# Joint expert tiles for two batches in a gated cross-attention and mixture-of-experts kernel

## The reference

```
x = x + tanh(g_xattn) * align(ctx, layernorm(x))          # x1
logits = layernorm(x1) @ gate_w.T
w, sel = top_k(logits, 2); w = softmax(w)
out = x1 + tanh(g_ffn) * sum_k w[k] * (layernorm(x1) @ expert_w[sel[k]].T)
```

## Time and profile before

| | |
|---|---|
| median of 3 runs | 618.98 us (618.24 to 619.47) |
| profiled execution | 618.64 us, its span 616.7 us |
| busy: PE, DVE, ACT, POOL | 492.8, 280.0, 280.7, 240.3 us |
| expert tiles | 78, gathers 277.8 to 588.6 us |

### The profile page before, as it was taken

How to read it: one execution, slowest core, us unless ns; L and a number is a source line. 1 busy time by engine, 2 the same in 40 slices (tenths; PEclk the granted TensorE clock), 3 DMA queues, 4 the chain that set the end, 5 groups by cost and what they waited for, 6 DMA issues and landing times.

```text
span 616.7 us, 7978 instructions
## 1 busy us (share of the span) xinstructions
PE 492.8 (80%) x2178; PEld 291.3 (47%) x2178; DVE 280.0 (45%) x1518; ACT 280.7 (46%) x525; POOL 240.3 (39%) x226
## 2 busy tenths in 40 slices
PE   7999565477133105889999999999999999999994
PEld 7999452345122102345455544444444444444442
DVE  6768799999988885997860400000000000000000
ACT  4548787844755403863665332222222222222221
POOL 4540130000000000003533657667667765766744
PEclk8999977667565656889998999999999999999998
DMA  8955335530073003378898667787778777877865
GB/s 295 358 170 167 94 74 158 134 94 2 0 269 141 2 1 142 136 261 273 290 350 217 119 111 134 134 160 134 125 137 160 133 142 143 129 140 140 158 106 64
DMA packets 56551, 92.42 MB, mean 150 GB/s; under 512 B 19013, under 2 KB 19269, under 8 KB 56349
## 3 DMA queue, kind: packets, MB, share of 16 engines
q0 software_dynamic: 17888, 41.95, 37.3%
q1 hardware_dynamic: 34093, 41.55, 20.1%
q10 hardware_dynamic: 4528, 8.41, 4.4%
HBM read 50.68 MB, written 41.21 MB: 149 GB/s over the span
## 4 chain that ended last, share of the span: by engine, by line
PE 57%; DVE 30%; DMA 6%; issue 3%; ACT 1%; POOL 1%; SPq 0%; POOLq 0%; ACTq 0%; DVEq 0%
PE psum L1793 43%; PE psum L1768 6%; DVE met L947 5%; DVE waves L861 5%; PE psum L1540 4%; DVE tokens L950 3%; DMA dist_rows<-work 3%; DVE tokens L885 3%; DVE shf L852 2%; DVE tokens L864 2%; DVE tokens L1012 2%; DVE tokens L855 2%; PE psum L1527 2%; DVE waves L851 1%; PE psum L1701 1%
## 5 line engine op out<-in xcount | busy, mean ns | idle before, releaser
L1793 PE MATMUL psum<-big,tokens 128*128 x616 | 278.7, 595 | 0.0
L1793 PEld LDWEIGHTS psum<-big,tokens 128*128 128x128 f32 x616 | 111.7, 191 | 111.5 <-issue 111.5
L659 POOL DMA_INDIRECT tokens<-x_rows,gather_ids x78 | 79.0, 1013 | 45.8 <-issue 40.0
L673 POOL DMA_INDIRECT out_dram<-work,add_ids x40 | 65.2, 1631 | 61.2 <-DMA out_dram<-work,add_ids 24.4
L1471 ACT ACTIVATE work<-psum,tile_shares 128x512 f32<-128x512 f32 x40 | 27.5, 687 | 105.3 <-PE psum L1793 95.0
L673 POOL DMA_INDIRECT out_dram<-prow,add_ids x37 | 58.5, 1582 | 42.4 <-issue 12.1
L1471 ACT ACTIVATE prow<-psum,tile_shares 128x512 f32<-128x512 f32 x37 | 25.4, 687 | 92.6 <-PE psum L1793 92.6
L687 POOL DMA_DIRECT2D out_dram<-tokens x1 | 1.0, 1031 | 160.8 <-DVE tokens L1012 160.8
L1591 PE MATMUL psum<-ident,stage 128*128 128x128 f32 x128 | 29.5, 421 | 35.3 <-ACT big L1355 20.2
L1768 PEld LDWEIGHTS psum<-ident,tokens 128*128 128x128 f32 x312 | 38.7, 141 | 39.4 <-issue 37.8
L1460 ACT COPY tokens<-psum 128x512 f32<-128x512 f32 x78 | 45.1, 578 | 13.2 <-PE psum L1768 8.5
(11 more groups left out here) (338 smaller groups left out, 668.7 us busy)
## 6 DMA issues: line engine op xcount, KB each, us to landing
tokens<-in_x_dram SPq DMA_DIRECT2D x16, 1024.0 KB, 11.1
stage<-in_L_ffn_expert_w_dram ACTq DMA_DIRECT2D x8, 1024.0 KB, 5.5
out_dram<-tokens SPq DMA_DIRECT2D x7, 1024.0 KB, 7.2
x_rows<-tokens SPq DMA_DIRECT2D x6, 1024.0 KB, 5.1
tokens<-dist_rows SPq DMA_DIRECT2D x52, 64.0 KB, 2.1
dist_rows<-work SPq DMA_DIRECT2D x16, 160.0 KB, 2.0
x_rows<-tokens SPq DMA_DIRECT2D x8, 256.0 KB, 4.3
dist_rows<-prow SPq DMA_DIRECT2D x5, 256.0 KB, 9.7
```

The lines of the kernel that those rows point to most:

```text
L659: pool.indirect_dma_start(out=xin[:, n % UX, :], out_offset=None, in_=x1_d[b][:, :], in_offset=bass.IndirectOffsetOnAxis(ap=gids[:, b, j:j ...
L673: pool.indirect_dma_start(out=out_d.rearrange("b t c -> (b t) c"), in_=yout(n), in_offset=None, out_offset=bass.IndirectOffsetOnAxis(ap=ai ...
L1793: ins = nc.tensor.matmul(psum[:, UP + n % UP, :], xinT[:, n % UX, c, :], expT[:, bass.ds(own, 1), c, :].rearrange("p o d -> p (o d)"), sta ...
```

## The change

Slots of the two batches are joined. First come `FA` = 9 tiles that hold only first choices of batch 0 and are full (whole multiples of 128 of an expert's first choices; the number 9 is the fewest there can be, (2048 − 8 x 127) / 128 rounded up). Everything else, the rest of batch 0's first choices, its second ones and both of batch 1, goes into one set of `JB` = 62 tiles. That makes 71 tiles in place of 78.

- The first tiles have tables of their own (`place_first`, `lay_first_lanes`, `lay_first_numbers`, `own_first`, `first_ids`), of 16 columns instead of 32, and need no pads. The second pick of batch 0 comes after their ids.
- The joint tables have 64 columns x 62 tiles; `place_choices` works on 512 columns, and `leave_first` takes out what the first tiles hold. They are made once, after nearly all contexts of batch 1.
- The shares of the joint tiles are not inverted. `x1_rows` is one tensor with rows of 514 numbers: x1 and the token's two shares. The shares are stored by `pairs_out` (2048 pieces of 8 bytes each for a batch, zeros before), and so come with the gather. Which of the two a slot needs is kept in `kinds`, and `tile_share(n)` (VectorE) makes the weights of each tile when it has been gathered. The first nine tiles' shares are still inverted.
- Up to three additions may be under way (`DEPTH`). Two joint tiles of one expert share no token. A tile that can share one with its two predecessors (an expert's first tile, an empty tile, and a last tile that is close behind batch 0's first choices) is marked by `mark_tiles`; SyncE's `clear(n)` reads the mark and gives GpSimd two permits for each tile, for a marked one only when both predecessors have landed.
- x of the last two groups of batch 1 is loaded earlier; gathered tiles lie in `stage`, not in `tokens`.

The core of the diff, with "..." where lines are left out:

```
...
-    AHEAD = 11
-    SEQ = [(0, j) for j in range(AHEAD)]
...
+    FA = -(-(T - E * (P - 1)) // P)
+    JB = (K * B * T - FA * P + E * (P - 1)) // P
+    KB = K * NT
+    NSEQ = FA + JB
...
+    DEPTH = 3
+    LAG = [min(n, 2, NSEQ - 1 - n) for n in range(NSEQ)]
...
+    RW = C + K
+    x1_d = nc.dram_tensor("x1_rows", (B * T, RW), F32, kind="Internal").ap()
...
+        SQUARED = [[], [], [16, 17], [18, 19, 20, 21], [22, 23, 24, 25], [26, 27, 28], [29, 30, 31]]
+        ALIGNED = [[], [18, 19], [20, 21], [22, 23, 24], [25, 26, 27], [28, 29, 30, 31]]
...
+            def pairs_out(b):
+                sp.wait_ge(s_pair, b + 1)
+                if b == 0:
+                    for n in range(FA - UX, FA):
+                        sp.wait_ge(s_xi[n % UX], 16 * (n // UX + 1))
+                sp.dma_start(x1_d[b * T:(b + 1) * T, C:RW].rearrange("(t p) k -> p t k", p=P),
+                             pairs[:, b * TB:(b + 1) * TB, :]).then_inc(s_sto[b], 16)
...
+            def clear(n):
+                if n == FA + 1:
+                    sp.wait_ge(s_mark, 1)
+                before = sp.value_load(flags[:, n - FA:n - FA + 1], min_val=0, max_val=16)
+                sp.wait_ge(s_add[(n - 1) % DEPTH], before + 16 * ((n - 1) // DEPTH))
+                sp.sem_inc(s_go, 1)
+                sp.wait_ge(s_add[(n - 2) % DEPTH], before + 16 * ((n - 2) // DEPTH))
+                sp.sem_inc(s_go, 1)
...
             def gather(n):
...
+                if n == FA:
+                    pool.wait_ge(s_ids, 2)
+                    for g in range(GB, NG):
+                        pool.wait_ge(s_rows[g], 16 * (GT if g == NG - 1 else 1))
+                    for b in range(B):
+                        pool.wait_ge(s_sto[b], 16)
...
             def add(n):
...
+                elif n >= DEPTH:
+                    pool.wait_ge(s_add[n % DEPTH], 16 * (n // DEPTH))
+                if n > FA:
+                    pool.wait_ge(s_go, 2 * (n - FA))
...
+            for n in range(NSEQ):
+                if n + UX == FA:
+                    while added < FA - 2:
+                        add(added)
+                        added += 1
...
+            def mark_tiles():
+                crossing = lv[0:1, 0:E]
...
+                lnk(v.scalar_tensor_tensor(crossing, ntl[0:1, :], float(P), spread(upto[0:1, TB - 1:TB], [[KB, E]]),
+                                           ALU.mult, ALU.subtract))
+                lnk(v.tensor_scalar(crossing, crossing, float(4 * P), -float(GONE), ALU.is_ge, ALU.mult))
+                lnk(v.tensor_tensor(crossing, crossing, lastt[0:1, :], ALU.add))
...
+                lnk(v.scalar_tensor_tensor(marks, tiles[0:1, :], tend[0:1, E - 1:E], marks, ALU.is_ge, ALU.max))
+                v.tensor_scalar(flags, marks, 16.0, None, ALU.mult).then_inc(s_mark, 1)
...
+            def tile_share(n):
+                j = n - FA
+                v.wait_ge(s_xi[n % UX], 16 * (n // UX + 1))
+                v.wait_ge(s_scale, n - FA + 1)
+                lnk(v.tensor_tensor(part_scale[:, :], xin[:, n % UX, C + 1:C + 2], kinds[:, 1, j:j + 1], ALU.mult))
+                v.scalar_tensor_tensor(scale[:, n:n + 1], xin[:, n % UX, C:C + 1], kinds[:, 0, j:j + 1], part_scale[:, :],
+                                       ALU.mult, ALU.add).then_inc(s_scale, 1)
...
```

VectorE's new order, and what changes in TensorE's:

```
+            logits(0); pick(0, 0); contexts 0..5; place_first(); contexts 6..9
+            lay_first_lanes(); contexts 10..12; lay_first_numbers(); contexts 13..15
+            own_first(); first_ids(); pick(0, 1); logits(1); scales(0); pick(1, 0)
+            pairs_of(0); lay_first_shares(); pick(1, 1); leave_first(); first_shares()
+            contexts 16..21; place_choices(); contexts 22..25; lay_lanes(0); lay_lanes(1)
+            contexts 26..28; pad_places(); lay_members(); lay_numbers(); contexts 29..31
+            pads(); scales(1); own_tiles(); ids(); pairs_of(1); mark_tiles()
+            for n in range(FA, NSEQ):
+                tile_share(n)
```

```
                 if n == 0:
-                    invert_shares(0)
+                    invert_first_shares()
                 if n == 1:
-                    count(1)
+                    count()
                 if n < len(ALIGNED):
                     for t in ALIGNED[n]:
                         align(t)
-                if n == 5:
-                    invert(1)
-                if n == 2:
-                    rank(1)
-                if n == 11:
-                    invert_shares(1)
+                if n == 3:
+                    rank()
+                if n == FA - 3:
+                    invert()
```

More of the change, by code:

```diff
@@ new lines, in lay_lanes @@
+            def lay_lanes(h):
+                if h == 0:
+                    v.wait_ge(s_out[1], 16)
+                    v.wait_ge(s_rows[1], 16)
+                    v.wait_ge(s_sq, 2 * GT)
+                else:
+                    v.wait_ge(s_invs, 1)
+                for q in range(2):
+                    v.tensor_tensor(lanes[h][:, :, q * TB:(q + 1) * TB], pattern,
+                                    spread(partf[:, 1, (2 * h + q) * TB:(2 * h + q) * TB + 1], [[0, P], [1, TB]]), ALU.is_equal)
@@ new lines, in lay_members @@
+            def lay_members():
+                for g in (2, 3):
+                    v.wait_ge(s_out[g], 16)
+                    v.wait_ge(s_rows[g], 16 * (GT if g == GB - 1 else 1))
+                v.wait_ge(s_sq, TB)
+                for q in range(KB // TB):
+                    ins = v.tensor_tensor(sets[:, 0, :, q * TB:(q + 1) * TB],
+                                          spread(partf[:, 0, q * TB:q * TB + 1], [[0, JB], [1, TB]]),
+                                          tilen[:, :, :], ALU.is_equal)
+                lnk(ins)
@@ L1166, in _, with ids @@
-            choose(0)
+            def ids():
+                v.wait_ge(s_inv, 2)
+                codes_ = psum[:, 7, JB:2 * JB]
+                later = owner
+                v.wait_ge(s_own, 2)
+                lnk(v.tensor_scalar(later, codes_, 0.0, float(B * T), ALU.is_lt, ALU.mult))
+                lnk(v.tensor_tensor(later, later, codes_, ALU.add))
+                ins = v.tensor_copy(rows_ids[:, FA:NSEQ], later)
+                for h in range(2):
+                    ins = v.tensor_scalar(hids[:, h:h + 1], later[:, JB - 1:JB], 2.0, float(h), ALU.mult, ALU.add)
+                ins.then_inc(s_ids, 1)
+                lnk(v.tensor_copy(kinds, bass.AP(psum[:, 7, 0:1].tensor, psum[:, 7, 0:1].offset,
+                                                 [psum[:, 7, 0:1].ap[0], [2 * JB, K], [1, JB]])))
@@ L1167, in _ @@
+            pick(0, 0)
             for t in range(0, 6):
                 add_context(t)
-            place_choices(0)
+            place_first()
             for t in range(6, 10):
                 add_context(t)
+            lay_first_lanes()
+            for t in range(10, 13):
+                add_context(t)
+            lay_first_numbers()
+            for t in range(13, TB):
+                add_context(t)
+            own_first()
+            first_ids()
+            pick(0, 1)
+            logits(1)
@@ L1172, in _ @@
+            scales(0)
+            pick(1, 0)
+            pairs_of(0)
+            lay_first_shares()
+            pick(1, 1)
+            leave_first()
+            first_shares()
+            for t in range(16, 22):
+                add_context(t)
+            place_choices()
+            for t in range(22, 26):
+                add_context(t)
             lay_lanes(0)
-            lay_numbers(0)
-            for t in range(10, TB):
+            lay_lanes(1)
+            for t in range(26, 29):
@@ L1192, in _ @@
-            pads(1)
-            own_tiles(1)
-            for t in (26, 27, 28):
-                add_context(t)
-            for t in (29, 30, 31):
-                add_context(t)
-            ids(1)
-            scales(1)
-            lay_shares(1)
-            shares_by_tile(1)
+            pad_places()
+            lay_members()
+            lay_numbers()
+            for t in range(29, NT):
+                add_context(t)
+            pads()
+            scales(1)
+            own_tiles()
@@ L1203, in _ @@
+            ids()
+            pairs_of(1)
+            mark_tiles()
+            for n in range(FA, NSEQ):
+                tile_share(n)
         @block.scalar
```

570 lines of the change are left out of this document (308 added, 262 removed).

## The result

The kernel after takes 620.7 us (median of 8 runs, 620.16 to 621.9), the kernel before on the same chip 618.82 (8 runs, 617.74 to 620.2): a ratio of 1.0033 (95% interval 1.002 to 1.0045), slightly slower. The forecast was 613.0, faster. The profiled execution after took 620.16 us for a span of 617.4; the seven others have spans of 618.6 to 620.2, so the profile is of the shortest of the eight.

A forecast was written before the change was run, and what follows sets the result against it. TensorE bounds the expert tiles, VectorE's order the part before 353 us. Tiles −27.1, start −2.2, tail +7.8 and about +15.5 for TensorE's longer road to product 8 gave 613 us, range 603 to 621.

The forecast's parts named there:

- Tiles and period: Expert tiles: 71 instead of 78 at 3.87 us each, −27.1 us; GpSimd's 3.17 us lies under that period.
- First product: Start of the kernel: first product moves from 283.4 to 281.2, −2.2 us, with the first gather at 275.5.
- Placing, and the wait at alignment 22: Before the joint tables: place_choices takes 8.7 us, to 307.0, and TensorE stands 5.6 us at alignment 22.
- VectorE's road: VectorE's chain through joint tables, last contexts, pads, owners, ids and pairs: share pairs ready at 338.5.
- The inversion: TensorE before product 7: 64 products take 4 us, from 2.8 for 32 narrower ones.
- TensorE's wait ahead of transposes 9: Before the joint stage: TensorE stands 10 us for gather 9, held by the pair store; product 8 ends at 355.1.
- The tail: After product 69 (T): the last three additions run in series at 5.55 us, end T + 19.4, against T + 11.6: +7.8 us.
- Outside the span: Around the profiled span of 610.7 us: 1.94 us more, giving 612.7.
- the gain is cancelled: Rival: VectorE's road is 5 to 8 us longer than drawn, time 618 to 621; chance 0.08.
- a slow pair store: Rival: the store of 2,048 8-byte pieces lands in 17 us instead of 6.5, time 623.5; chance 0.12.
- a slower gather: Rival: rows of 2,056 bytes raise the gather from 0.98 to 2 us, period 4.2, time 633; chance 0.05.
- No stand at tile 9, a cheap tail: Rival: no TensorE wait before tile 9 (600.5), or end additions landing in 3 us (606); chance 0.18 for one.

The follow-up runs named there:

- Rows together: Kernel after with the joint tables laid out so the 124 numbers an inversion product streams are adjacent, not 128 bytes apart: 616.84 us, 0.9976.
- the steps of 32 bytes: Kernel after with joint tables in four blocks of 16 positions, so streamed numbers lie 32 bytes apart instead of 128: 621.33 us, 1.005.
- the pairs first: Kernel after with VectorE's pairs_of(1) moved ahead of own_tiles and the ids: 613.73 us, 0.9928.
- the empty tiles aside: Kernel after with additions of tiles 69 and 70, empty for these inputs, sent to two scratch tensors without waiting: 612.45 us, 0.9906.
- the five edits of order and layout: Kernel after with adjacent numbers, pairs before ids, earlier tables and squares, product 8 before transposes 9, pair store before the last 1 MB output store: 606.3 us.
- four of them and the empty tiles aside: Kernel after with adjacent numbers, pairs before ids, earlier tables and squares, product 8 before transposes 9, additions 69 and 70 to scratch tensors: 602.42 us, 0.9758.
- the same move of the tables: Kernel after with choices placed, tables laid and inversion run earlier: 622.82 us; with ScalarE's squares of tiles 26 to 31 also beside tile 5: 615.87 us.
- four edits together: Kernel after with adjacent numbers, pairs before ids, earlier tables and squares, and product 8 before transposes 9: 609.4 us, 0.9872.

## Why the prediction was wrong

- **Tiles and period: right.** 71 gathers; from 360.72 to 596.95 are 61 periods, 236.23 us, 236.2 in the sum. GpSimd needs 3.18 us a tile.
- **First product: right.** It starts at 281.02, 281.2 in the sum; the first gather at 275.13, 275.5.
- **Placing, and the wait at alignment 22: right.** Placing from 299.19 to 307.5 (298.25 to 307.0); TensorE stands 5.31 us (5.6); product 6 ends at 329.56 (329.0).
- **VectorE's road: right.** Numbers ready at 329.3 (329.1), context 31 at 331.3 (331.2), pads at 334.0 (334.2), owners at 336.6 (336.5). Without a wait it would have been through the pairs by 338.5, as the sum has it.
- **The inversion: wrong, and this is the step that failed.** "64 products, 4 us, from the 2.8 for 32 narrower ones" rests on no rule: by the number of products alone the 2.8 would have given 5.6, and by the numbers streamed (32 x 39, 2.2 ns each) 17.8 us for 64 x 124. It took 14.0, 1.8 ns a number. What I should have set beside it is the share inversion of before (below), whose numbers are adjacent: 32 products of 117 in 2.14 us, 0.57 ns a number. Rows together shows the difference on one kernel (5.4 us for 14.0), and the steps of 32 bytes show that the distance isn't what counts. It isn't the clock either (the windows below this list).
  The Trainium skill ("Advanced Engine Details and Errata", SBUF Cachelines) says that on-chip memory is read in lines of 16 bytes, and that there is a penalty when each access falls into another line; by it, steps of 32, 64 and 128 bytes should all pay and adjacent numbers not. The runs agree; no run tried a step below 16 bytes.
- **What followed from it.** Ten us more of inversion made the pairs 7.9 us late (346.4 for 338.5), since they stood behind the ids; with the pairs first the store was issued at 337.56. From store to gather took 5.3 us (6.5), and gather to transposes 3.45 (3.6). Product 8 ended at 360.72 instead of 355.1, 5.6 us late. TensorE's wait ahead of transposes 9 was there, but of 4.86 us and not some 10: the long inversion had put product 7 off too, to 350.1 instead of 338.6.
- **The tail: right in kind, 1.0 short.** With T = 596.95 the additions start at T − 0.9, + 4.7, + 10.1 (− 0.9, + 4.9, + 10.8), but from the last half's start to the end are 8.5 us, not 6.7 as before. It is 8.5 to 8.7 in all eleven kernels with the change, those with the empty tiles aside among them; why stays open. Empty tiles aside confirms the steps.
- **Outside the span: right for most executions.** In the profiled one 2.8 us lie outside it, 1.9 in the sum; in the seven others it is 1.7 to 2.0, and their spans are 1.2 us longer or more.

The share inversion in TensorE's timeline of the kernel before:

```profile
286.87 2.14 PE L1746 MATMUL psum<-tokens,stage 128*128 128x117 bf16 x32
```

Two windows of the inversion in the kernel after, at either level of the granted clock (1.00 is 2.4 GHz, 0.50 is 1.2), with 11 products in 2.0 us and 20 in 3.7, the same pace:

```profile
332.00:334.00 2.00, 2.00 (x11) 1.29 (x10) 1.93 (x9) 1.98 (x3) 0.00 (x0) 1.00 1.06 350
...
340.00:343.70 3.70, 3.70 (x20) 2.47 (x19) 0.00 (x0) 0.00 (x0) 0.00 (x0) 0.50 0.00 0
```

Of the miss of 7.7 us (620.7 for 613.0), the profiled execution shows 5.6 from the inversion, by way of the order ids, then pairs, and 1.0 from the tail. The last 1.1 can't be placed: the other executions have longer spans, and no profile shows where. With the 5.6 us off, the time would be about 615.1, faster than before: the sign hung on the first term. The time is in the range of the rival "the gain is cancelled", but not by its mechanism: VectorE's road wasn't longer; VectorE stood waiting for TensorE. The rivals of a slow pair store and a slower gather fell: 4.4 us to land, and 0.98 us a gather. No stand at tile 9, a cheap tail: neither came of itself, and both could be had, as the pairs first and the empty tiles aside show. By the packet figure of the Trainium skill ("DMA: Bandwidth & Descriptors", Measured) the estimate for the pair store was 21.5 us. The trace disagrees: 4.4 us, and 6.9 and 8.7 only with other stores in the way.

With these costs mended the change is faster than the kernel before: 606.3 us, 2%, with the five edits of order and layout, which use nothing of the inputs; 602.42 with four of them and the empty tiles aside, which do use them. The kernel before was given no such edits: what it would gain from adjacent numbers in its own inversions (2.80 us for 32 products) or from another order was not run.

## What to carry to other kernels

Price a product by the numbers that it streams and by whether they lie side by side, and take the price from a row with the same layout. A table is best laid out for its reader when the reader goes through it many times, though the writer's cost is then on the road too (here 4.1 us, against 8.7 won). Where an engine runs in a fixed order, move up whatever doesn't need the result of the coming wait, on all engines at once: the same move of the tables lost 2 us or won 4, depending on one line of ScalarE's order. Additions that have to follow each other cost a whole landing each, 5.6 us, and at the end of a kernel nothing covers that, so work that is known to be empty shouldn't be in such a chain.

## What was unexpected in the hardware

- A product of 124 f16 numbers takes 0.22 us when they are 128 bytes apart and 0.24 at 32 bytes, at either level of the clock. With adjacent numbers it takes 0.07 at a granted 1.00 (four edits together, 2.19 us for 32), and 0.10 in the second half of rows together, at a mean of 0.62 (3.10 us for 32).
- The granted clock can be at its lower level, 1.2 GHz (0.50), while TensorE counts as busy 6.73 of 6.73 us with such products; product 7 behind them still took 5.24 us. In the kernel with the four edits, where the inversion took 4.1 us, the product behind it took 3.60.
- 2,048 pieces of 8 bytes landed in 4.4 us in the kernel after, with nothing else issued by SyncE for 13 us, and in 6.9 and 8.7 when the last store of x1 had been issued 2.8 us before.
